# Another order of the attention step in stages 1 and 2 of a four-layer transformer kernel

## What is computed

```python
q = heads(LN(x) @ wq.T + bq)
k = heads(ctx @ wk.T + bk)
v = heads(ctx @ wv.T + bv)
scores = einsum('bhld,bhsd->bhls', q, k) / sqrt(8)   # layer 2: masked positions at -inf
out = einsum('bhls,bhsd->bhld', softmax(scores), v)
x = x + out                                          # layer 2: x + (out @ w_o.T + b_o)
```

## Time and profile before

| what | before |
|---|---|
| median of 3 runs | 904.42 us (903.49 to 904.74) |
| the profiled execution | 902.79 us, span 901.0 us |
| PE, DVE busy | 586.1 us (65%), 572.2 us (64%) |
| ACT, POOL busy | 386.0 us (43%), 284.3 us (32%) |
| mean granted clock of PE | 0.776 |
| attention 1, first to last copy into `shift_t` | 320.69 to 411.89 us |
| attention 2, second to last copy | 559.12 to 655.45 us |

### The profile page before, as it was taken

One profiled execution on the slowest core, in us unless ns is written; L12 is line 12 of the kernel. 1 busy time (PEld: TensorE's weight loads), 2 busy tenths in 40 slices (PEclk: granted clock), 3 DMA queues, 4 the chain that ended last, 5 costly groups with the idle time before them and its releaser, 6 DMA issues.

```text
span 901.0 us, 19762 instructions
## 1 busy us (share of the span) xinstructions
PE 586.1 (65%) x5767; PEld 400.7 (44%) x5772; DVE 572.2 (64%) x1842; ACT 386.0 (43%) x873; POOL 284.3 (32%) x614
## 2 busy tenths in 40 slices
PE   5599999977888688785133227999941588522321
PEld 3478787864444455552011114666621365311111
DVE  2576767644777476776888844666665433377774
ACT  1356555533222256664266654555520245232332
POOL 2211111203555433331242263243110333345440
PEclk9899999987999668987555557999965589755555
DMA  8333322210000133430000021333200355100001
GB/s 250 93 67 66 69 60 59 55 36 1 0 0 0 36 80 98 105 93 14 0 0 0 1 52 36 95 83 86 64 9 0 88 132 146 47 0 1 0 0 47
DMA packets 103974, 46.73 MB, mean 52 GB/s; under 512 B 84144, under 2 KB 93424, under 8 KB 103920
## 3 DMA queue, kind: packets, MB, share of 16 engines
q1 hardware_dynamic: 103920, 46.09, 20.5%
HBM read 26.13 MB, written 19.92 MB: 51 GB/s over the span
## 4 chain that ended last, share of the span: by engine, by line
PE 31%; issue 20%; DVE 16%; POOL 8%; DVEq 6%; DMA 6%; POOLq 6%; ACT 4%; SPq 2%; ACTq 1%
DMA scratch_q<-q_parts 3%; PE bank L462 2%; POOL small L1234 2%; DMA stacks<-scratch_q 2%; PE bank L420 2%; PE bank L479 2%; PE bank L583 2%; PE bank L396 2%; PE bank L414 2%; PE bank L555 1%; PE bank L596 1%; PE bank L509 1%; DVE small L1304 1%; PE bank L431 1%; SPq L355 1%
## 5 line engine op out<-in xcount | busy, mean ns | idle before, releaser
L1472 DVE TENSOR_REDUCE mx<-bank 128x4 f32<-128x512 f32 x160 | 103.9, 684 | 24.7 <-PE bank L420 22.8
L850 ACT ACTIVATE probs<-bank 128x512 f32<-128x512 f32 x160 | 90.9, 595 | 56.9 <-PE bank L441 51.8
L1114 POOL TENSOR_TENSOR stats<-stats,half_neg 128x1 f32<-128x1 f32 x64 | 35.2, 549 | 197.2 <-DVE stats L1443 189.9
L792 PE MATMUL bank<-ident_bf,yq 128*128 128x128 bf16 x16 | 4.6, 286 | 68.5 <-DVE yq L1866 68.5
L1454 DVE TENSOR_TENSOR x_sb<-bank,x_sb 128x128 f32 (+1 forms) x64 | 18.5, 289 | 45.8 <-PE bank L583 22.7
L479 PE MATMUL bank<-probs,v_slot 128*9 128x128 f32 x1024 | 44.8, 290 | 3.1 <-ACT probs L850 0.4
L1487 DVE SCALAR_TENSOR_TENSOR resid<-bank,w_bias_cols,q_parts 128x128 f32<-128x128 f32 x48 | 16.8, 350 | 46.9 <-ACT q_parts L896 46.9
L1165 POOL CAST q_parts<-resid 128x128 bf16<-128x128 f32 x48 | 14.2, 296 | 97.9 <-DVE resid L1487 97.9
L504 PE MATMUL bank<-w_ident,xn 128*128 128x128 f32 x64 | 21.9, 342 | 32.3 <-DVE xn L1448 21.4
L882 ACT ACTIVATE xn_t<-bank 128x128 f32<-128x128 f32 x64 | 17.7, 277 | 56.6 <-PE bank L504 55.0
L437 PE MATMUL bank<-stacks 48*128 48x128 bf16 x512 | 40.8, 233 | 1.5 <-DVE shift_t L1508 1.2
(11 more groups left out here) (288 smaller groups left out, 1805.3 us busy)
## 6 DMA issues: line engine op xcount, KB each, us to landing
stacks<-scratch_k SPq DMA_DIRECT2D x64, 96.0 KB, 2.2
stacks<-scratch_q SPq DMA_DIRECT2D x64, 96.0 KB, 2.2
scratch_k<-k_parts SPq DMA_DIRECT2D x48, 96.0 KB, 1.8
scratch_q<-q_parts SPq DMA_DIRECT2D x48, 96.0 KB, 1.9
scratch_k<-k_parts SPq DMA_DIRECT2D x48, 64.0 KB, 1.7
scratch_q<-q_parts SPq DMA_DIRECT2D x48, 64.0 KB, 1.8
stacks<-scratch_k SPq DMA_DIRECT2D x16, 192.0 KB, 2.7
stacks<-scratch_q SPq DMA_DIRECT2D x16, 192.0 KB, 2.4
```

The lines of the kernel that those rows point to most:

```text
L850: activation(probs[:, slot, :], bank[2 + u % 2][:, :], ACT.Tanh if layer == 3 else ACT.Exp, scale=float(d) ** -0.5).then_inc(sm["p"], 1)
L1114: tt(stats[:, s, 9:10], stats[:, s, 8:9], half_neg[:, :], ALU.pow).then_inc(ln_rstd, 1)
L1472: reduce(mx[:, sM, at * UNIT:(at + 1) * UNIT], bank[u % 2][:, :].rearrange("p (h k) -> p h k", h=UNIT), AX.X, ALU.max).then_inc(sm["mx"], 1)
```

## The change

Seven moves in the steps of attentions 1 and 2, and one in SP's program. On PE `M(0)` comes to the head of the step, `turn_xn` ahead of `ST(0)`, `query` ahead of `M(1)`. On ACT `xn_turned` and `query` each come one place earlier. On DVE `shifts_turned` goes behind `maximum(1)`, and `q_rest` ahead of `maximum(3)`. SP writes part 0 of the query on `q_h` and the two others on `parts`.

```diff
@@ SP, stacks @@
-                    sp.wait_ge(sm["parts"], t + 1)
+                    sp.wait_ge(sm["q_h"], t + 1)
                     row = 0
                     for part, n in TERMS:
+                        if part == 1:
+                            sp.wait_ge(sm["parts"], t + 1)
                         sp.dma_start(scratch_q[s, row:row + n].rearrange("j r k -> r j k"),
@@ PE, attention_step @@
                     elif layer < 3:
+                        if Mo: M(0)
                         if Do: AV(2, 1); AV(3, 1)
                         if Po: shift_turn()
-                        if Mo: M(0)
+                        if A: turn_xn()
                         if Po: ST(0)
                         if Do: out_turn()
-                        if A: turn_xn()
+                        if A: query()
                         if Mo: M(1)
-                        if A: query()
                         if Do and layer == 2: att_turn()
@@ ACT, attention_step @@
                         values_out()
+                        xn_turned()
                         probabilities(0)
-                        xn_turned()
+                        query()
                         probabilities(1)
-                        query()
                         out_turned()
@@ DVE, attention_step @@
                     elif layer < 3:
-                        shifts_turned()
                         maximum(0)
                         maximum(1)
+                        shifts_turned()
                         statistics_ahead()
                         normalized()
                         maximum(2)
+                        q_rest()
                         maximum(3)
                         shifts()
-                        q_rest()
                         out()
```

## The result

| | median | profiled execution |
|---|---|---|
| before | 904.23 us (4 runs) | 902.79 us, span 901.0 |
| after | 927.12 us (923.50 to 927.99, 4 runs) | 923.5 us, span 921.7 |
| ratio | 1.0246, interval 1.0217 to 1.0275 | +20.7 us |

What follows compares the result with a forecast made beforehand. Attention 2 was taken as bound by PE, attention 1 by no engine's busy time. Attention 2 +12.7 and attention 1 +2.4 made +15.1 us, on the median 919.5 us, 1.7% slower; range 906 to 933 us.

Steps and rivals of the forecast that it cites:

- The ring in attention 2: Attention 2, every step: PE idles before `ST(0)` while `M(0)`, two maxima and copy run; 0.94 us, fifteen steps +14.1 us.
- The heads in attention 2: Attention 2, k = 4, 8, 12: about 0.5 of the 1.0 us extra is given back, three times, -1.4 us.
- The ordinary step of attention 1: Attention 1 at full clock: the loop through PE and DVE sums to 5.7 us a step, in twelve steps.
- the sum of its chain: Attention 1, from `q_rest` to `M(0)`: 6.66 us falls to 6.17, so the query's stack comes in time.
- The heads and the clock in attention 1: Attention 1: three steps with statistics at 6.9 us, three steps at low clock +4.5 us; the stage in all +2.4 us.
- The Trainium skill's rule on the clock: Attention 1: by this rule, waits cut into smaller pieces would keep the full clock, and the stage comes out at -2.1 us.
- A: Slower rival: clock lost in six steps of attention 2 and seven of attention 1; about 935 us; chance 0.13.
- B: Faster rival: PE's other work covers attention 2's wait, attention 1 loses its stack waits; -12, about 892 us; chance 0.09.
- C: Cancelling rival: attention 1 gains 12 us, attention 2 loses 12.7; about 905 us; chance 0.10.

Runs made afterwards that it cites:

- copy_between: The changed kernel with DVE's copy into `shift_t` moved between maximum 0 and maximum 1; 917.47 us, ratio 1.0172 to the kernel before.
- copy_behind: The kernel before with only DVE's copy into `shift_t` moved behind maximum 1; 957.34 us, ratio 1.0608.
- after_again: The changed kernel measured once more, unaltered; 925.21 us, ratio 1.0231 to the kernel before.
- after_fill: The changed kernel with 24 unused products on PE where it stands for `xn` at k = 4, 8, 12; 918.39 us, ratio 1.0163 to before.
- q_early: The kernel before with only SP's split query writes and `q_rest` ahead of `maximum(3)`; 902.60 us, ratio 1.0005.
- q_pool: q_early with POOL held back until DVE's shifts are done; 903.96 us, ratio 1.0004 to the kernel before.

## Why the prediction was right or wrong

1. *The ring in attention 2: right.* Sum of the step 7.56, measured 7.49; PE's wait 0.94, measured 0.68 in the record of `ST(0)`, and 0.87 by the length of the step. 2.55 us from `M(0)` to `ST(0)`, measured 2.45. copy_between and copy_behind show that it is this ring: one maximum less in it, 0.48 us less; no cover beside it, 1.51 us of waiting. Two of the fifteen steps did not grow by it, though all were counted: the third (7.36 before, 7.49 after) and the last (6.34 and 6.44).
2. *The heads in attention 2: wrong by some 2 us.* I gave back 0.5 of the 1.0 us that two steps around a head took over ordinary ones. In the new order they take 7.64 and 8.60 from `shift_turn` to `shift_turn`, 1.26 over two of 7.49. Nothing is given back. Items 1 and 2 together: +11.8 for +12.7. That it is so near is in part luck: the 1.5 us of the two steps that did not grow and the 2 us of the heads stand against each other.
3. *The ordinary step of attention 1: right.* 5.7 forecast, 5.55 measured, and the wait for the stack down from 6.4 to 1.5 us, nearly gone, as the sum of its chain said. The sum went through DVE alone. A second chain closes at the same place, from `ST(0)` through ACT's exponentials to `ST(1)`, the value groups and `M(0)`, which starts at 375.01, 0.1 behind the end of maximum 3 at 374.91; the prediction had no wait on it, and it held 8.0 us of PE's. Which of the two sets the step is not shown.
4. *The heads and the clock in attention 1: the terms that were mis-sized.* +2.4 forecast, +5.9 measured, and +9.7 in after_again. Two terms. A head was put at 1.2 us over an ordinary step; with most of the clock kept (after_fill) two steps around a head take 13.25, 2.1 over two ordinary ones: 2.7 us more than forecast for the three. With it goes that attention 1 was to gain 2.1 us at full clock, and loses 1.0 with the fill. What I had left out stands on DVE between maximum 3 and the statistics:

```profile
379.78 0.68 DVE L1474 TENSOR_REDUCE mx<-bank 128x4 f32<-128x512 f32 x1
380.56 0.37 DVE L1502 TENSOR_SCALAR shift<-mx 128x16 bf16<-128x16 f32 x1
381.00 0.18 DVE L1504 SCALAR_TENSOR_TENSOR shift<-mx,shift 128x16 bf16<-128x16 f32 x1
381.82 0.29 DVE L1441 BATCH_NORM_STATS2 stats<-x_sb 128x6 f32 x1 [0.64 <-issue]
```

   From 380.46 to 381.82 it is 1.36 us, not the 0.56 that I set for the shifts: 0.2 more for the slow shift, 0.64 of standing for nothing that the profile shows. PE's stand for `xn` was put at 1.5 to 1.7 us and was 2.68. The other term is the clock: 4.5 us were taken, three steps of 1.5, and the clock did fall at all three heads, k = 4, 8 and 12. By after_fill it cost 5 us in one profiled execution, as forecast, and 9 in the other, twice that.
5. *The edges of the stages: left out.* 3.0 us, mostly ahead of the first `shift_turn` of each stage; 1.1 of them were there before the orders differ.
6. *The Trainium skill's rule on the clock* ("TensorE: Matmul & The Clock Gate", "What's actually happening"), that activity releases the slow clock: my reading of it, that the waits would be cut into smaller pieces and keep the clock, did not come true: PE's longest stand grew, from 1.34 us in the earlier trace rows to 2.68, and attention 1 ran at 0.84. What it says of activity agrees with the runs: 1.5 us of unused products in that stand, and the clock was 0.95.
7. *The rivals.* A (ring and a lost clock) was nearest where the result left the forecast, but for attention 1 alone; in attention 2 the clock is 0.97 in both kernels. B and C need a cover of 2.55 us beside the ring; it was 1.6 by the step's length (2.45 less 0.87), as the sum had it.

The profiled execution of after is the quickest of its four runs, 923.5 us at a mean granted clock of 0.780; the others took 926.5, 927.8 and 928.0 us at 0.772, 0.775 and 0.769. So the distance between its +20.7 and the medians' +22.9 goes with the clock; that it was lost in attention 1 is likely by after_again, and not shown for these three.

## What to carry to other kernels

Where two engines hand work to and fro, an instruction put earlier on one of them pulls into its wait all that stands ahead of its partner on the other: add up the ring (here `M(0)`, two maxima, copy, `ST(0)`), subtract what the waiting engine can do meanwhile, and the remainder is paid in every step. A chain that is made shorter pays only if the next one is not as long; q_early removed 6.0 of 6.4 us of waits and gained nothing. Where PE stands longest once in a few steps, its clock can cost as much as the stand (here 6.5 us at three heads, and 5 or 9 us that the fill took back), and a few products without use can be cheaper than none. To say what a change costs in clock, give the kernel before the same help and compare again.

## What the runs showed of the hardware

DVE's `TENSOR_SCALAR` of 128x16 from SBUF to SBUF takes 174 ns with POOL at rest and 370 when a `TENSOR_TENSOR` of POOL has just begun. Timeline of DVE in q_early, and POOL behind it:

```profile
366.01 0.37 DVE L1502 TENSOR_SCALAR shift<-mx 128x16 bf16<-128x16 f32 x1
```

```profile
365.92 0.43 POOL L1169 TENSOR_TENSOR q_parts<-resid,q_parts 128x128 bf16<-128x128 f32 x1
```

POOL ends at 366.35, DVE at 366.38: the short instruction waited for the long one. The Trainium skill, "SBUF — State Buffer", section "Who interferes with whom", says that GpSimd and a VectorE instruction in a two-port mode take one port pair in turn, each for a whole instruction; the rows agree, and q_pool with all 32 back at 174 to 176 ns shows that POOL's instruction is the cause; that it is the ports, no row shows.

DVE's statistics in attention 2 wait for a semaphore that the DVE instruction right before them raised. They start 0.53 us after its end in before and 0.49 after the change (`[0.49 <-DVE x_sb L1456]`), with no other instruction of DVE in the rows between.
